# Gate and up products of the experts with features along the partitions, for all 256 rows of a block at once

## What is computed

```
x_flat = x.reshape(-1, 512)                                  # 4096 tokens
topk_weights, topk_indices = top_k(x_flat @ router_w + router_b, k=2)
topk_weights = softmax(topk_weights)
# the 8192 (token, expert) pairs are sorted by expert
ff_gate = ragged_dot(sorted_tokens, we_gate, group_sizes)    # 512 x 512 for each expert
ff_up   = ragged_dot(sorted_tokens, we_up, group_sizes)
ff_out  = ragged_dot(silu(ff_gate) * ff_up, we_down, group_sizes) * sorted_weights
output[sorted_token_idx] += ff_out
```

## Time and profile before

| | us |
|---|---|
| three runs | 2869.32, 2870.94, 2877.44 |
| median | 2870.94 |
| the profiled execution | 2874.91 |
| its span in the trace | 2873.2 |
| TensorE busy over the span | 2665.0 (93%) |
| DVE, ACT, GpSimd busy over the span | 2000.5 (70%), 1620.8 (56%), 1468.0 (51%) |
| mean granted TensorE clock | 0.973 of full speed |

### The profile page before, as it was taken

One profiled execution on the slowest core, in us unless ns is written; L12 is line 12 of the kernel. 1 busy time (PEld: TensorE's weight loads), 2 busy tenths in 40 slices (PEclk: granted clock), 3 DMA queues, 4 the chain that ended last, 5 costly groups with the idle time before them and its releaser, 6 DMA issues. The chain is left out here.

```text
span 2873.2 us, 48962 instructions
## 1 busy us (share of the span) xinstructions
PE 2665.0 (93%) x15375; PEld 2267.7 (79%) x15375; DVE 2000.5 (70%) x4223; ACT 1620.8 (56%) x3157; POOL 1468.0 (51%) x1676
## 2 busy tenths in 40 slices
PE   7999989999899999899998599999959999999997
PEld 5888878888788888788887487877748888888886
DVE  6777766777667777677777688978846556666655
ACT  3666666666656666566666333333336666666665
POOL 3676646676647675556565333434323444343434
PEclk9999999999999999999999799999979999999999
DMA  6654544444544444444444654544334443444433
GB/s 175 106 122 106 123 103 98 118 113 104 132 96 99 115 107 114 103 109 100 94 91 114 170 135 134 158 134 147 96 126 96 102 87 74 102 99 100 100 52 51
DMA packets 192360, 316.56 MB, mean 110 GB/s; under 512 B 60496, under 2 KB 106224, under 8 KB 189104
## 3 DMA queue, kind: packets, MB, share of 16 engines
q1 hardware_dynamic: 148656, 216.86, 31.6%
q0 software_dynamic: 43520, 97.46, 13.9%
HBM read 241.08 MB, written 75.17 MB: 110 GB/s over the span
## 5 line engine op out<-in xcount | busy, mean ns | idle before, releaser
L1095 ACT ACTIVATE a_pt<-a_PT 128x512 fp32r<-128x512 f32 (+3 forms) x768 | 350.4, 491 | 449.9 <-PE a_PT L962 443.3
L1226 DVE TENSOR_TENSOR a_pt<-a_PT,a_pt 128x512 fp32r<-128x512 f32 (+3 forms) x768 | 401.5, 550 | 155.2 <-ACT a_pt L1095 150.7
L1216 DVE CUSTOM_DVE_ANT_0 a_S<-a_S,a_mask 128x1024 f32<-128x1024 f32 (+7 forms) x512 | 387.5, 757 | 72.5 <-PE a_S L951 71.1
L1084 ACT ACTIVATE a_pb<-a_S,a_nmax 128x1024 f32<-128x1024 f32 (+7 forms) x512 | 381.0, 744 | 36.5 <-DVE a_nmax L1216 36.5
L962 PE MATMUL a_PT<-early_ident,a_pb 128*128 128x128 f32 x2304 | 345.0, 276 | 51.2 <-DVE a_pt L1226 50.9
L962 PEld LDWEIGHTS a_PT<-early_ident,a_pb 128*128 128x128 f32 x2304 | 275.9, 142 | 112.4 <-issue 58.5
L979 PE MATMUL a_O<-a_pt,a_v 128*128 128x256 f32 (+1 forms) x2560 | 346.5, 283 | 17.8 <-DVE a_xt L1201 16.8
L979 PEld LDWEIGHTS a_O<-a_pt,a_v 128*128 128x128 f32 x2560 | 330.4, 193 | 31.2 <-DVE a_xt L1201 24.0
L2193 DVE TENSOR_TENSOR e_w<-early_stage,e_w 128x1024 fp32r<-128x1024 f32 x238 | 280.6, 1220 | 65.0 <-ACT e_w L2142 64.9
L950 PE MATMUL a_S<-a_kh,a_qs 128*128 128x512 f32 (+3 forms) x768 | 286.7, 373 | 10.6 <-DMA a_kl<-a_rot 8.8
L951 PE MATMUL a_S<-a_kl,a_qs 128*128 128x512 f32 (+3 forms) x768 | 259.0, 349 | 0.0
(11 more groups left out here) (305 smaller groups left out, 6890.2 us busy)
## 6 DMA issues: line engine op xcount, KB each, us to landing
a_qs<-a_rot SPq DMA_DIRECT2D x256, 128.0 KB, 2.4
a_kh<-a_rot SPq DMA_DIRECT2D x256, 128.0 KB, 2.4
a_kl<-a_rot SPq DMA_DIRECT2D x256, 128.0 KB, 2.4
e_rows<-scr_hs SPq DMA_DIRECT2D x40, 516.0 KB
scr_attT<-a_ot SPq DMA_DIRECT2D x256, 64.0 KB, 2.2
m_att<-scr_attT SPq DMA_DIRECT2D x32, 512.0 KB
m_rb<-scr_rinv SPq DMA_DIRECT2D x64, 256.0 KB
early_stage<-in_wqk POOLq DMA_DIRECT2D x31, 512.0 KB
```

The source lines that it names most:

```text
L1084: act.activation(pb[u % 2][:, 0:cols], S[u % 2][:, 0:cols], ACT.Exp, bias=nmax[:, u % GU:u % GU + 1], scale=-1.0, accum_out=rsum[:, b % 2, ...
L1095: act.activation(pt[u % 2][:, 0, 4 * s:4 * s + m, (qt % 2) * P:(qt % 2 + 1) * P], PT[(k + s) % 2][:, 0:m * P].rearrange("p (k q) -> p k q" ...
L1216: dve.tensor_tensor_reduce(out=sc, in0=sc, in1=mask[:, T - cols:T], scale=-1.0, scalar=-MASKED, op0=ALU.add, op1=ALU.min, accum_out=nmax[: ...
L1226: dve.tensor_tensor(pt[u % 2][:, 1, 4 * s:4 * s + m, q], PT[(k + s) % 2][:, 0:m * P].rearrange("p (k q) -> p k q", k=m), pt[u % 2][:, 0, 4 ...
```

## The change

- Gate and up are made with the weights as the stationary operand (128 features by 128 features at a time) and the transposed rows of both tiles, 256 columns, as the moving one. The result has features along the partitions. `product(j, k, out, h, sem)` makes two of the four feature slices into one bank, so h is a half of the features, and gate and up take 96 products of 256 columns a block where they took 48 of 512.
- The activation comes out in the layout that down needs. `turn_act` and its semaphore go. `act_high` and `act_low` read a32 (SBUF) in place of pT[0] (PSUM). hT, sil, a32 and aT are laid out anew, with the same number of elements.
- `turn_rows` uses pT[0] and pT[1] for its two tiles, and waits for the turn_low two back in place of the one just before.
- `down(j, t, h)` adds up one half of the features; each tile takes two calls. TensorE's order is gate 0, gate 1, up 0, up 1, down 0 first half, turn_rows 0, down 1 first half, turn_rows 1, down 0 second half, down 1 second half.
- ACT: weight_high of the next gate weights moves ahead of act_high(0), act_high(1) directly behind it; turn_high(1) moves ahead of weight_high of the up weights and row_out(0).
- DVE: the wait for "added", the copy of dest, the gate arithmetic and keep_side move ahead of mult(0); turn_low(1) moves ahead of the two halves of the up weights.
- GpSimd: fetch(0) moves ahead of the wait for the first row copy and add_rows(0).

```diff
@@ -1973,10 +1973,10 @@
         gate = rm.sb("gate", [P, RT])
         wt = rm.sb("wt", [P, RT])
         dest = rm.sb("dest", [P, RT], I32)
-        hT = rm.sb("hT", [P, RT, 2, D], F32R)
-        sil = rm.sb("sil", [P, RT, D])
-        a32 = rm.sb("a32", [P, RT, D])
-        aT = rm.sb("aT", [P, RT, 2, D], F32R)
+        hT = rm.sb("hT", [P, 2, ET, BLK], F32R)
+        sil = rm.sb("sil", [P, 2, 2 * BLK])
+        a32 = rm.sb("a32", [P, 2, 2 * BLK])
+        aT = rm.sb("aT", [P, 2, ET, BLK], F32R)
         y = rm.sb("y", [P, RT, D])
         ident = route["ident"]
         part = rm.sb("part", [P, 1], I32)
@@ -1987,7 +1987,7 @@
         ix = rm.sb("ix", [P, 3], I32)
         pT, pG, pU, pY = ([rm.ps(f"{n}{i}", [P, 512]) for i in range(2)] for n in "TGUY")
 
-        names = ("any padded rows raw0 raw1 raw2 whi0 whi1 whi2 wlo0 wlo1 wlo2 Th thi tlo Ta ahi alo G U sil mul "
+        names = ("any padded rows raw0 raw1 raw2 whi0 whi1 whi2 wlo0 wlo1 wlo2 Th thi tlo ahi alo G U sil mul "
                  "Y y st0 st1 added nxt side arg gate wt part src ix").split()
         s = {k: rm.sem(k) for k in names}
         CR = 2
@@ -2046,11 +2046,11 @@
                 for k in range(3):
                     wait_alone(gp, s[f"raw{k}"], 16 * j + 16, s["any"])
                 point(j + 2)
-                wait_alone(gp, s["y"], 2 * j + 1 + CR, s["any"])
-                add_rows(0)
                 wait_alone(gp, s["ix"], j + 2, s["any"])
                 wait_alone(gp, s["wlo0"], 2 * j + 4, s["any"])
                 fetch(0)
+                wait_alone(gp, s["y"], 2 * j + 1 + CR, s["any"])
+                add_rows(0)
                 wait_alone(gp, s["y"], 2 * j + 2 + CR, s["any"])
                 add_rows(1)
                 wait_alone(gp, s["wlo1"], 2 * j + 4, s["any"])
@@ -2071,55 +2071,50 @@
 
             def turn_rows(j, t):
                 pe.wait_ge(s["rows"], 16 * (j + 1))
-                pe.wait_ge(s["tlo"], 2 * j + t + CR)
+                pe.wait_ge(s["tlo"], 2 * j + t - 1 + CR)
                 for e in range(ET):
-                    mm = pe.transpose(pT[1][:, e * P:(e + 1) * P], rows[:, t, e * P:(e + 1) * P], ident[:, :])
+                    mm = pe.transpose(pT[t][:, e * P:(e + 1) * P], rows[:, t, e * P:(e + 1) * P], ident[:, :])
                 mm.then_inc(s["Th"], 1)
 
-            def turn_act(j, t):
-                pe.wait_ge(s["mul"], 2 * j + t + 1 + CR)
-                pe.wait_ge(s["alo"], 2 * j + t + CR)
-                for f in range(ET):
-                    mm = pe.transpose(pT[0][:, f * P:(f + 1) * P], a32[:, t, f * P:(f + 1) * P], ident[:, :])
-                mm.then_inc(s["Ta"], 1)
-
-            def product(j, k, out, t, sem):
-
-                if t == 0:
+            def product(j, k, out, h, sem):
+
+                if h == 0:
                     pe.wait_ge(s[f"wlo{k}"], 2 * j + 2)
                 if k == 0:
-                    pe.wait_ge(s["tlo"], 2 * j + t + 1 + CR)
-                    pe.wait_ge(s["mul"], 2 * j + t - 1 + CR)
-                for e in range(ET):
-                    mm = parts(out[t][:, :], lambda a: hT[:, t, a, e * P:(e + 1) * P],
-                               lambda a: w[:, k, a, e * D:(e + 1) * D], e)
+                    pe.wait_ge(s["tlo"], 2 * j + RT + CR)
+                    pe.wait_ge(s["mul"], 2 * j + h - 1 + CR)
+                for f in range(2 * h, 2 * h + 2):
+                    for e in range(ET):
+                        c = e * D + f * P
+                        mm = parts(out[h][:, f % 2 * BLK:(f % 2 + 1) * BLK], lambda a: w[:, k, a, c:c + P],
+                                   lambda a: hT[:, a, e, :], e)
                 mm.then_inc(s[sem], 1)
 
-            def down(j, t, f0, f1):
-                if f0 == 0:
-                    pe.wait_ge(s["alo"], 2 * j + t + 1 + CR)
+            def down(j, t, h):
+
+                pe.wait_ge(s["alo"], 2 * j + h + 1 + CR)
+                if h == 0:
                     pe.wait_ge(s["y"], 2 * j + t - 1 + CR)
-                    if t == 0:
-                        pe.wait_ge(s["wlo2"], 2 * j + 2)
-                for f in range(f0, f1):
-                    mm = parts(pY[t][:, :], lambda a: aT[:, t, a, f * P:(f + 1) * P],
+                    pe.wait_ge(s["wlo2"], 2 * j + 2)
+                for f in range(2 * h, 2 * h + 2):
+                    mm = parts(pY[t][:, :], lambda a: aT[:, a, f, t * P:(t + 1) * P],
                                lambda a: w[:, 2, a, f * D:(f + 1) * D], f)
-                return mm
+                if h == 1:
+                    mm.then_inc(s["Y"], 1)
 
             for t in range(RT):
                 turn_rows(0, t)
             with pe.Fori(0, NBLK) as j:
                 product(j, 0, pG, 0, "G")
+                product(j, 0, pG, 1, "G")
                 product(j, 1, pU, 0, "U")
-                product(j, 0, pG, 1, "G")
-                turn_act(j, 0)
                 product(j, 1, pU, 1, "U")
+                down(j, 0, 0)
                 turn_rows(j + 1, 0)
-                down(j, 0, 0, 2)
-                turn_act(j, 1)
-                down(j, 0, 2, ET).then_inc(s["Y"], 1)
+                down(j, 1, 0)
                 turn_rows(j + 1, 1)
-                down(j, 1, 0, ET).then_inc(s["Y"], 1)
+                down(j, 0, 1)
+                down(j, 1, 1)
 
         @block.scalar
         def _(act):
@@ -2127,13 +2122,15 @@
 
             def turn_high(j, t):
                 act.wait_ge(s["Th"], 2 * j + t + 1)
-                act.wait_ge(s["U"], 2 * j + t - 1 + CR)
-                act.activation(hT[:, t, 0, :], pT[1][:, :], ACT.Copy).then_inc(s["thi"], 1)
-
-            def act_high(j, t):
-                act.wait_ge(s["Ta"], 2 * j + t + 1)
-                act.wait_ge(s["Y"], 2 * j + t - 1 + CR)
-                act.activation(aT[:, t, 0, :], pT[0][:, :], ACT.Copy).then_inc(s["ahi"], 1)
+                act.wait_ge(s["U"], 2 * j + CR)
+                act.activation(hT[:, 0, :, t * P:(t + 1) * P], pT[t][:, :].rearrange("p (e r) -> p e r", e=ET),
+                               ACT.Copy).then_inc(s["thi"], 1)
+
+            def act_high(j, h):
+                act.wait_ge(s["mul"], 2 * j + h + 1 + CR)
+                act.wait_ge(s["Y"], 2 * j + CR)
+                act.activation(aT[:, 0, 2 * h:2 * h + 2, :], a32[:, h, :].rearrange("p (f r) -> p f r", f=2),
+                               ACT.Copy).then_inc(s["ahi"], 1)
 
             def weight_high(j, k, done):
                 if not isinstance(j, int):
@@ -2141,9 +2138,9 @@
                 act.wait_ge(s[done], 2 * j + CR)
                 act.activation(w[:, k, 0, :], raw[:, k, :], ACT.Copy).then_inc(s[f"whi{k}"], 1)
 
-            def silu(j, t):
-                act.wait_ge(s["G"], 2 * j + t + 1 + CR)
-                act.activation(sil[:, t, :], pG[t][:, :], ACT.Silu).then_inc(s["sil"], 1)
+            def silu(j, h):
+                act.wait_ge(s["G"], 2 * j + h + 1 + CR)
+                act.activation(sil[:, h, :], pG[h][:, :], ACT.Silu).then_inc(s["sil"], 1)
 
             def row_out(j, t):
                 act.wait_ge(s["Y"], 2 * j + t + 1 + CR)
@@ -2158,16 +2155,16 @@
             with act.Fori(0, NBLK) as j:
                 silu(j, 0)
                 silu(j, 1)
+                weight_high(j + 1, 0, "G")
                 act_high(j, 0)
-                weight_high(j + 1, 0, "G")
+                act_high(j, 1)
                 turn_high(j + 1, 0)
                 act.wait_ge(s["arg"], j + 1)
                 act.activation(gate[:, :], arg[:, :], ACT.Tanh).then_inc(s["gate"], 1)
-                act_high(j, 1)
+                turn_high(j + 1, 1)
                 weight_high(j + 1, 1, "U")
                 act.wait_ge(s["wt"], j + 1)
                 row_out(j, 0)
-                turn_high(j + 1, 1)
                 row_out(j, 1)
                 weight_high(j + 1, 2, "Y")
 
@@ -2179,13 +2176,15 @@
 
             def turn_low(j, t):
                 dve.wait_ge(s["thi"], 2 * j + t + 1)
-                dve.tensor_tensor(hT[:, t, 1, :], pT[1][:, :], hT[:, t, 0, :].bitcast(F32),
-                                  ALU.subtract).then_inc(s["tlo"], 1)
-
-            def act_low(j, t):
-                dve.wait_ge(s["ahi"], 2 * j + t + 1)
-                dve.tensor_tensor(aT[:, t, 1, :], pT[0][:, :], aT[:, t, 0, :].bitcast(F32),
-                                  ALU.subtract).then_inc(s["alo"], 1)
+                c = slice(t * P, (t + 1) * P)
+                dve.tensor_tensor(hT[:, 1, :, c], pT[t][:, :].rearrange("p (e r) -> p e r", e=ET),
+                                  hT[:, 0, :, c].bitcast(F32), ALU.subtract).then_inc(s["tlo"], 1)
+
+            def act_low(j, h):
+                dve.wait_ge(s["ahi"], 2 * j + h + 1)
+                f = slice(2 * h, 2 * h + 2)
+                dve.tensor_tensor(aT[:, 1, f, :], a32[:, h, :].rearrange("p (f r) -> p f r", f=2),
+                                  aT[:, 0, f, :].bitcast(F32), ALU.subtract).then_inc(s["alo"], 1)
 
```

(20 more changed lines are left out.)

## The result

The kernel after takes 2909.7 us (median of four runs, 2908.5 to 2913.2), the kernel before, on the same chip, 2871.6. The ratio is 1.0131, with an interval of 1.0119 to 1.0143: slower by 38 us, where 15 us faster was forecast. The profiled execution has a span of 2911.5 us, against 2873.2.

A forecast was written before the change was run, and what follows sets the result against it. The prediction took TensorE's stream to bound the kernel. Plain blocks -17.0 us, seven loading blocks +3.3, the start -1.0: -14.7, so 2870.9 - 15 = 2856 us; own range 2847 to 2862 (chance 0.41), full range 2838 to 2886.

The forecast's parts named there:

- rival 4: TensorE's weight loads are not hidden: 40 more a block at 0.14 to 0.19 us, about 3130 us; chance 0.02.
- Its length is the open cost: GpSimd's first scatter in a block: 2.61 or 1.63 us long in the earlier trace, taken as 1.62.
- the prediction's loop: Row copy, two scatters, landing, DVE's wait, first multiplication, next down product: closes at 17.55 us, or 18.14 with serial scatters.
- S: Start of a block's first down product on TensorE, from which the prediction counts all times in the block.
- the extra on fetch(0): GpSimd's one extra microsecond a block put on fetch(0), so it ends at S + 7.70, the first scatter starts at S + 8.01.
- rival 3: Scatter loop with long first scatter and serial landing: block 18.66, slower from 9.03 us row copy to "added"; 2888 us; chance 0.17.
- rival 1: The scatter loop doesn't bind and TensorE's shorter stream shows in full, 28.5 us and some waits: 2840 us; chance 0.20.
- The serial landing: The two scatters' transfers, some 2.5 us each, run one after the other: second lands 5.7 us after the first one's issue.
- rivals 2 and 3: Scatter loop takes the gain back, seven loading blocks at 20.5: no change, 2869 us (chance 0.20), or slower, 2888 (0.17).
- bound and threshold: TensorE's stream of 17.81 us against the scatter loop's 17.55 or 18.14, within 0.4; slower above 9.03 from row copy to "added".
- the 14 of the loading blocks: The seven blocks that load another expert's weights, at 20.5 us each, add 14 us in the rivals' sums.
- the 1.0 of the start: TensorE's idle time ahead of the first up product, 1.0 us, which the first block may lose.

The follow-up runs named there:

- e1: Kernel after with DVE's wait for "added" and the small operations behind it moved back behind the block's last act_low: 2845.6 us, ratio 0.9913.
- e4: Kernel after with weight_low of the up and down weights cut to 8 columns of each half: 2858.2 us (one run).
- e3: Kernel after with ACT's first row copy ahead of weight_high of the up weights: 2862.3 us, ratio 0.9959.
- e5: Kernel after with GpSimd's fetch(0) between the two scatters again: 2994.8 us, ratio 1.0440.
- e9: Kernel before with DVE's wait for "added" moved ahead of mult(0), and up and down weight subtractions cut to 8 columns a half: 2946.2 us, ratio 1.0254.
- e7: Kernel after with weight_low in pieces of half the length, the same work: 2868.5 us, ratio 0.9990.
- e8: Kernel after with fetch(0) between the scatters again, and up and down weight subtractions cut to 8 columns a half: 2937.1 us, ratio 1.0222.
- e2: Kernel before with only DVE's wait for "added" and the small operations behind it moved ahead of mult(0): 2978.9 us, ratio 1.0378.

## Why the prediction was wrong

**What held.** The bound of the kernel before was TensorE's stream. The 256-column product costs 0.118 (2400.86, 2400.98, 2401.10; 95 of them in a row in 11.24), the weight loads are hidden, and the new stream is 17.83 (e1) where 17.81 was predicted. That settles rival 4: the page "TensorE: Matmul & The Clock Gate" of the Trainium skill, section "The mechanism", has a rule that would have left the loads of full-height products exposed, and the rows speak against it here. (The same section also lets a load into the background weight buffer run ahead, which would fit; no run here shows which buffer a load uses.) The changed wait was named as the place where the gain could go, with the engines behind it, and DVE does wait for "added" in every block. The reactions held too: 0.85 from row copy to scatter, 0.30 between scatters.

**The step that failed** is "Its length is the open cost", the first scatter, and with it the length inside the landing of the second. Both bounds were read in the earlier trace rows, 1.63 and 2.61. I took 1.62, because I ascribed the long form to GpSimd's idle time, with "about one GpSimd instruction a block" as a budget that fetch(0) would use up. The correlation was real in the kernel before (seven of seven), but its cause was DVE, and nothing limits holds to one in a block: the change puts both scatters behind the row copy while DVE subtracts the up and then the down weights. Term by term, against the 17.55 of the prediction's loop:

- the row copy ends at S + 6.94 for 6.69: +0.25
- the extra on fetch(0) doesn't come (1.02 long): -0.47
- first scatter 2.48 for 1.62: +0.86
- second scatter's issue 2.62 for 1.75: +0.87
- from the end of its issue to DVE's destination copy 3.46 for 3.12: +0.34
- the destination copy to the next S 3.01 for 2.74: +0.27
- the gap between the scatters 0.30 for 0.31: -0.01

17.55 + 2.11 = 19.66. The two holds are 1.7 of it. Without them e4 takes 2858.2, 2 us from the forecast of 2856.0. That is closer than the forecast deserves: e4's plain blocks average 17.9 for its 18.0, its seven loading ones 19.6 for 19.0, and the two errors nearly cancel. The other terms are 0.4 together, about what the forecast's 18.0 had allowed over 17.55.

**The size.** The forecast's mean interval was (31 x 18.0 + 7 x 19.0) / 38 = 18.18; measured 19.51. 38 x 1.33 = 50.5 of the 53.7 us by which the time was missed. The other 3 are at the ends: I gave the start 1.0 us back and it is 3.3 later, and the end is 1.2 shorter.

**The rivals.** Rival 3 was the right one, by its mechanism and by its threshold: row copy to "added" above 9.03 us means slower; it is 9.64 (2409.38 to 2419.02, 0.07 before the destination copy). But it took the long form for the first scatter only, so its block was 18.66 instead of 19.5. Its sum is 2888, and the range stops at 2886, short of its own rival; at the other end, rival 1's 2840 with 0.1167 a product is 2835, not 2838. Neither changes the outcome. The serial landing of rival 3 isn't seen: the second scatter lands 2.8 to 3.8 us after the end of its issue in all blocks of after, for the 3.1 of a plain block before, and no run shows the 2.5 us of transfer that this landing was worked out with. The seven loading blocks were feared at 20.5 in rivals 2 and 3. In the slower loop they are nearly covered: behind the first block only three intervals between destination copies exceed 19.7, and the longest is 20.86, where the clock is at 0.83 in the two microseconds behind 2.01 us of idle time and at 0.50 in the next two.

**The chance.** I wrote that bound and threshold were 0.4 us apart and still gave 0.17 to slower, because I had chosen the short scatter and then ranged over everything else. The unknown was the same for both scatters, so the case "both long" belonged in the list: 17.55 - 0.47 + 1.0 + 0.87 = 18.95, or 0.42 a block over 18.53, x 32 = 13, and with the 14 of the loading blocks and the 1.0 of the start 2897: above the range, and still 13 below what was measured.

## What to carry to other kernels

When a wait is moved ahead of work that feeds the bounding engine, close the loop through it with every duration at its long end, and compare with the stream: 0.4 us of slack was less than one unexplained duration. A duration that comes in two lengths wants its cause before it is used; lay the rows of all engines for that moment side by side, not only those of its own queue. And a change made of two parts is best timed apart: here the moved wait took 64 us, and all the rest gave 25.

## What the runs showed of the hardware

- An indirect DMA issued by GpSimd (scatter or load) that starts while DVE subtracts with both operands in SBUF is recorded longer, until 1.5 us (scatter) or 0.9 us (load) behind that instruction's end: up to 2.67 us for 1.60 (scatter, e3), up to 2.09 for 1.04 (load, e5). Behind a DVE instruction with one operand in PSUM it isn't (1.62 to 1.64 for a scatter, e9; 0.99 to 1.01 for a load, before). The hold isn't longer than one DVE instruction: pieces of half the length cut it to 0.4 (e7), and cost DVE 2.50 for 2.36 for the same columns.
- A scatter behind an indirect megabyte load lands late. With 0.3 us from the end of the load's issue to the scatter it lands 5.7 to 7.4 us behind the end of its own issue for 3.3 (e8), and 6.2 to 7.8 in the kernel before; with 3.0 to 4.2 us 4.0 to 6.2 (e4); with 3.9 to 4.0 us 3.2 to 3.8 (the kernel after). The distance isn't all: in e5, where the load's own issue was held, it is 4.4 to 4.7 at 0.3.
- TensorE's granted clock is 0.50 in the windows behind idle times of 4.66 and 4.97 us, and a 512-column product then takes 0.43 us for 0.233. In e2 this lasts six microseconds, so the stall is paid for twice. At idle times around 2 to 3 us both levels occur, and what decides is open.
